# A graph-attention kernel: two result banks in turn, split operands for the small sums, and an earlier low part on GpSimd

## The reference

```python
# first layer (H is 1024 nodes x 64 hyperedges, 0 or 1; a node is in about 3)
h = x @ W
alpha = softmax(where(H.T > 0, leaky_relu(h @ a_node)[:, None, :], -1e9), -1)
agg = einsum('ben,bnf->bef', alpha, h)
beta = sigmoid((h @ a_gn)[:, None, :] + (agg @ a_ge)[:, :, None])
all_he = elu(beta[..., None] * h[:, None] + (1 - beta[..., None]) * agg[:, :, None])
se = tanh(elu(agg) @ fcW + fcb) @ av
coefs1 = softmax(where(H > 0, se[:, None, :], -1e9), -1)
g = einsum('bne,benf->bnf', coefs1, all_he)
...
# third layer (w: a 3 x 64 x 64 weight for each of 16 embedding directions)
w = einsum('nd,dkio->nkio', embedding, weight)
x_g = einsum('knm,bmc->bnkc', A_stack, x)
out = einsum('bnki,nkio->bno', x_g, w) + embedding @ bias
```

## Time and profile before

| | |
|---|---|
| median of 3 runs | 732.07 us |
| profiled execution | 729.97 us, of which 728.2 us is the span |
| TensorE busy | 665.5 us (91%) |
| VectorE, ScalarE, GpSimd busy | 421.7, 337.2, 289.7 us |
| first round starts, last round ends | about 102.8 us, 195.8 us |
| third layer's products (L1503) | 490.6 to 643 us |

### The profile page before, as it was taken

How to read it: one execution, slowest core, us unless ns; L and a number is a source line. 1 busy time by engine, 2 the same in 40 slices (tenths; PEclk the granted TensorE clock), 3 DMA queues, 4 the chain that set the end, 5 groups by cost and what they waited for, 6 DMA issues and landing times.

```text
span 728.2 us, 9826 instructions
## 1 busy us (share of the span) xinstructions
PE 665.5 (91%) x3420; PEld 460.7 (63%) x3428; DVE 421.7 (58%) x970; ACT 337.2 (46%) x645; POOL 289.7 (40%) x267
## 2 busy tenths in 40 slices
PE   6898988878799889999999999999999989899993
PEld 2796766656566767533333358887776767678883
DVE  1676656777439942466877856114565757561166
ACT  1861234544367442356566544413446565355214
POOL 0270105565526810001424257024667676760045
PEclk9999999999989799999999999999999999999998
DMA  9120030000000036000100000000000000000013
GB/s 329 34 87 2 1 116 1 1 0 1 2 1 1 4 79 153 1 0 1 59 0 1 1 1 1 1 0 1 2 1 1 0 1 1 1 1 2 1 28 88
DMA packets 14995, 18.34 MB, mean 25 GB/s; under 512 B 10128, under 2 KB 10128, under 8 KB 14944
## 3 DMA queue, kind: packets, MB, share of 16 engines
q1 hardware_dynamic: 14432, 16.06, 7.7%
q10 hardware_dynamic: 512, 1.60, 0.6%
HBM read 11.37 MB, written 2.10 MB: 18 GB/s over the span
## 4 chain that ended last, share of the span: by engine, by line
PE 53%; DVE 7%; POOL 7%; ACT 3%; issue 2%; ACTq 0%; POOLq 0%; DVEq 0%
PE PS L1503 8%; PE PS L1390 7%; PE PS L1373 7%; PE PS L1516 5%; PE PS L1556 4%; PE PS L1545 4%; POOL LN_Y L163 3%; DVE arena L2139 2%; PE PS L182 2%; PE PS L1482 2%; PE PS L1489 2%; PE PS L189 2%; PE PS L1566 2%; DVE LN_ST L140 2%; PE PS L1252 1%
## 5 line engine op out<-in xcount | busy, mean ns | idle before, releaser
L2139 DVE SCALAR_TENSOR_TENSOR arena<-PS,WT,arena 128x256 f32<-128x256 f32 x160 | 77.4, 484 | 59.2 <-PE PS L1516 34.6
L1713 ACT ACTIVATE arena<-PS,spare 128x1024 f32<-128x1024 f32 x64 | 70.8, 1109 | 49.8 <-DVE spare L2076 49.6
L1503 PE MATMUL PS<-WH,KK 128*128 128x512 f32 x256 | 87.2, 404 | 6.1 <-POOL KK L1917 5.6
L2076 DVE TENSOR_REDUCE spare<-PS 128x1 f32<-128x1024 f32 x64 | 75.6, 1219 | 23.8 <-PE PS L1373 23.7
L163 POOL TENSOR_TENSOR LN_Y<-LN_V,CN 128x16 f32<-128x16 f32 (+1 forms) x18 | 49.4, 2745 | 73.7 <-DVE LN_V L155 73.7
L1781 ACT ACTIVATE spare<-PS,WT 128x256 f32<-128x256 f32 x96 | 38.8, 472 | 68.5 <-DVE arena L2139 66.7
L1873 POOL TENSOR_TENSOR arena<-arena,spare 128x128 f32<-128x128 f32 x32 | 13.9, 433 | 134.7 <-DVE spare L2082 124.0
L1390 PE MATMUL PS<-arena 128*64 128x512 f32 x256 | 62.0, 605 | 1.5 <-POOL arena L1873 1.4
L1503 PEld LDWEIGHTS PS<-WH,KK 128*128 128x128 f32 x256 | 48.0, 188 | 24.0 <-issue 12.4
L1503 PE MATMUL PS<-WL,KK 128*128 128x512 f32 x128 | 50.1, 391 | 0.0
L1373 PE MATMUL PS<-arena 64*128 64x512 f32 x192 | 48.2, 618 | 1.4 <-ACT arena L1713 1.4
(11 more groups left out here) (293 smaller groups left out, 1491.8 us busy)
## 6 DMA issues: line engine op xcount, KB each, us to landing
arena<-in_adj_tr SPq DMA_DIRECT2D x8, 512.0 KB, 5.8
arena<-in_x_tr SPq DMA_DIRECT2D x4, 512.0 KB, 7.9
arena<-in_x_nat SPq DMA_DIRECT2D x1, 2048.0 KB, 9.2
arena<-arena SPq DMA_DIRECT2D x7, 256.0 KB, 2.8
arena<-arena SPq DMA_DIRECT2D x12, 128.0 KB, 2.3
spare<-in_w SPq DMA_DIRECT2D x2, 512.0 KB, 4.1
out<-arena SPq DMA_DIRECT2D x4, 256.0 KB, 3.0
out<-arena SPq DMA_DIRECT2D x8, 128.0 KB, 2.2
```

What stands on the lines that cost most here:

```text
L1503: ins = pe.matmul(acc, x[:, t % 2, b, :], w[:, k, c], start=(first and n == 0), stop=(not first and n == 2), skip_group_check=True)
L1713: act.activation(EF[2 * (i % RING) + par], banks("S", 2 * i + par).rearrange("p a c -> p (a c)"), ACT.Exp, bias=NMX[:, i, par:par + 1], ac ...
L2076: dve.tensor_reduce(NMX[:, i, par:par + 1], banks("S", 2 * i + par), AX.XY, ALU.max, negate=True).then_inc(max_ready, 1)
L2139: dve.scalar_tensor_tensor(acc, PS[:, four_banks(t, j), d * F:(d + 1) * F], WT[:, e:e + 1], acc, ALU.mult, ALU.add).then_inc(acc_step, 1)
```

## The change

It has five parts. (1) The sums of a tile go to bank 4 or 7 in turn (`sums_bank`), and TensorE waits for the copy of the tile before last. The denominators move to bank 5 and are added up round by round: ScalarE copies them to `ZR` when the round is done, GpSimd adds `ZR` to `ZS`. (2) In a round, `gather(t, C_)` comes ahead of `edge_rows`, and VectorE shifts chunk A ahead of `from_first`. (3) `small_sums` uses float32r operands with high and low part side by side (`SMR`, `HMR`): six products of 36 and 32 columns, whose halves are added by a `tensor_reduce`. (4) `NSF` becomes a float32r tile. (5) In the third layer's loop `low_parts(t + 1)` is issued ahead of `scales`.

```diff
-        NSF = arena[:, 4 * SLOT + CHUNKS * BF:4 * SLOT + CHUNKS * BF + ROUND].rearrange("p (c n) -> p c n", n=P)
+        NSF = rounded("NSF", 4 * SLOT + CHUNKS * BF, [P, CHUNKS, P])
...
+        SMR = nc.alloc_sbuf_tensor_at("SMR", [P, 2, 18], F32R, offset=spare_at + 4 * (2 * N + ROUND))
+        HMR = nc.alloc_sbuf_tensor_at("HMR", [P, NT, 2, 16], F32R, offset=spare_at + 4 * (2 * ROUND))
...
-        SMALL_AT, ZN_AT = CHUNKS * E, 0
+        SMALL_AT, ZN_AT = CHUNKS * E, 3 * P
+        ZR = sb("ZR", [P, B])
+        zr_out, zs_added = sem("zr_out"), sem("zs_added")
+
+        def sums_bank(t):
+            return 4 + 3 * (t % 2)
+
...
+        def small_parts(c):
+            return PS[:, 5, SMALL_AT + 36 * c:SMALL_AT + 36 * c + 36].rearrange("p (h k) -> p h k", k=18)
...
+                        pool.wait_ge(zr_out, j + 2)
+                        pool.tensor_tensor(ZS[:, t, :], ZS[:, t, :], ZR[:, :], ALU.add).then_inc(zs_added, 1)
                     if t + 2 < NT:
                         low(t + 2)
                     if t >= 1:
...
+                act.activation(ZR[:, :], zero16[:, 0:B], ACT.Copy).then_inc(zr_out, 1)
...
+                        act.wait_ge(acc_done, j + 2)
+                        act.activation(ZR[:, :], PS[:, 5, ZN_AT:ZN_AT + B], ACT.Copy).then_inc(zr_out, 1)
                     if t + 2 < NT:
                         high(t + 2)
-                    act.wait_ge(acc_done, first[t + 1] + 1)
-                    act.activation(GN[:, t, :], PS[:, 4, :], ACT.Copy)
-                    act.activation(ZS[:, t, :], PS[:, 7, ZN_AT:ZN_AT + B], ACT.Copy).then_inc(acc_out, 1)
+                    act.activation(GN[:, t, :], PS[:, sums_bank(t), :], ACT.Copy).then_inc(acc_out, 1)
...
+                    parts = PS[:, 5, SMALL_AT:SMALL_AT + 36 * CHUNKS].rearrange("p (c h k) -> p c h k", h=2, k=18)[:, :, :, 0:17]
+                    dve.tensor_reduce(TS[:, :, :], parts.rearrange("p c h k -> p c k h"), AX.X, ALU.add).then_inc(ts_ready, 1)
...
+                link(dve.tensor_copy(SMR[:, :, 17:18], zero16[:, 0:2].unsqueeze(2)))
+                link(dve.tensor_copy(SMR[:, 0, 0:17], SM[:, :]))
+                dve.tensor_tensor(SMR[:, 1, 0:17], SM[:, :], bits(SMR[:, 0, 0:17]), ALU.subtract)
...
-                ins.then_inc(hm_ready, 1)
+                link(ins)
+                dve.wait_ge(hg_out, 1)
+                link(dve.tensor_copy(HMR[:, :, 0, :], HM[:, :, 0:2 * B]))
+                dve.tensor_tensor(HMR[:, :, 1, :], HM[:, :, 0:2 * B], bits(HMR[:, :, 0, :]), ALU.subtract).then_inc(hm_ready, 1)
...
+                        shift(A_, 2)
                         dve.wait_ge(selg_ready, j + 1)
                         dve.wait_ge(nt_ready, j + 1)
                         from_first(at).then_inc(ns_half, 1)
-                        shift(A_, 2)
...
-                        dve.wait_ge(acc_out, t)
+                        dve.wait_ge(zs_added, first[t])
...
+                dve.wait_ge(zs_added, first[NT])
...
+                        acc = small_parts(c)
+                        pe.matmul(acc, SELF[:, c, :], SMR[:, :, :], start=True, stop=False, skip_group_check=True)
+                        ins = pe.matmul(acc[:, :, 0:16], NSF[:, c, :], HMR[:, bass.ds(t, 1), :, :].rearrange("p t h k -> p (t h) k"),
+                                        start=False, stop=True, skip_group_check=True)
...
-                    if t >= 1:
-                        pe.wait_ge(acc_out, t)
-                    pe.matmul(PS[:, 4, :], zero16[:, 0:P], zero16[:, :], start=True, stop=False, skip_group_check=True)
-                    pe.matmul(PS[:, 7, ZN_AT:ZN_AT + B], zero16[:, 0:P], zero16[:, 0:B], start=True, stop=False, skip_group_check=True)
+                    if t >= 2:
+                        pe.wait_ge(acc_out, t - 1)
+                    pe.matmul(PS[:, sums_bank(t), :], zero16[:, 0:P], zero16[:, :], start=True, stop=False, skip_group_check=True)
                     pe.wait_ge(hpl_ready, min(t + 2, NT))
                     with pe.Fori(first[t], first[t + 1]) as j:
                         k_next, t_next = next_round(j, t, first)
 
...
-                            return pe.matmul(PS[:, 4, :], NST[:, c, :], S1[:, c, :], start=False, stop=True, skip_group_check=True)
-
+                            return pe.matmul(PS[:, sums_bank(t), :], NST[:, c, :], S1[:, c, :], start=False, stop=True, skip_group_check=True)
+
+                        pe.wait_ge(z_ready, CHUNKS * j + 1)
+                        gather(t, C_)
+                        pe.wait_ge(zr_out, j + 1)
                         pe.wait_ge(ns_ready, j + 2)
                         edge_rows(t_next)
-                        pe.wait_ge(z_ready, CHUNKS * j + 1)
-                        gather(t, C_)
                         pe.wait_ge(nst_out, j + 1)
...
-                            ins = pe.matmul(PS[:, 7, ZN_AT:ZN_AT + B], NST[:, c, :], CC[:, c, :], start=False, stop=True,
-                                            skip_group_check=True)
+                            ins = pe.matmul(PS[:, 5, ZN_AT:ZN_AT + B], NST[:, c, :], CC[:, c, :], start=(c == 0),
+                                            stop=(c == CHUNKS - 1), skip_group_check=True)
                         ins.then_inc(acc_done, 1)
...
                     add_scaled(t, 0)
+                    if t + 1 < NT:
+                        low_parts(t + 1)
                     for i, (first, n) in enumerate(NORMS):
                         if first + n == t:
                             scales(i)
                     if t + 1 < NT:
-                        low_parts(t + 1)
                         init(t + 1)
                     add_scaled(t, 1)
                     combine(t)
```

More of the change, by code:

```diff
@@ L353, in _ @@
                 pool.memset(zero16[:, :], 0.0).then_inc(zero_set, 1)
+                pool.memset(ZS[:, :, :], 0.0)
                 pool.wait_ge(sl, 1)
@@ L497, in nodes_copy @@
                 def nodes_copy():
-                    act.activation(NSG[:, :, :], NSF[:, :, :], ACT.Copy).then_inc(nsg_ready, 1)
+                    act.activation(NSG[:, :, :], bits(NSF[:, :, :]), ACT.Copy).then_inc(nsg_ready, 1)
                 def tanh():
@@ L622, in to_last @@
                 def to_last(at):
-                    return dve.scalar_tensor_tensor(NSF[:, :, :], iota, HIT[:, bass.ds(at, 1)], NSF[:, :, :], ALU.is_lt, ALU.mult)
+                    return dve.scalar_tensor_tensor(NSF[:, :, :], iota, HIT[:, bass.ds(at, 1)], bits(NSF[:, :, :]), ALU.is_lt, ALU.mult)
                 def edges(k):
@@ L632, in small_out @@
                 def small_out():
-                    dve.tensor_copy(TS[:, :, :], PS[:, 5, SMALL_AT:SMALL_AT + 17 * CHUNKS].rearrange("p (c k) -> p c k", k=17)).then_inc(ts_ready, 1)
+                    parts = PS[:, 5, SMALL_AT:SMALL_AT + 36 * CHUNKS].rearrange("p (c h k) -> p c h k", h=2, k=18)[:, :, :, 0:17]
+                    dve.tensor_reduce(TS[:, :, :], parts.rearrange("p c h k -> p c k h"), AX.X, ALU.add).then_inc(ts_ready, 1)
                 def logits():
@@ L924, in edge_rows @@
                     for c in range(CHUNKS):
-                        ins = pe.matmul(PS[:, 5, c * E:(c + 1) * E], NSF[:, c, :], P1[:, bass.ds(t, 1), :], start=True, stop=True)
+                        ins = pe.matmul(PS[:, 5, c * E:(c + 1) * E], bits(NSF[:, c, :]), P1[:, bass.ds(t, 1), :], start=True, stop=True)
                     ins.then_inc(r_ready, 1)
@@ L929, in turn_nodes @@
                     for c in range(CHUNKS):
-                        ins = pe.transpose(PS[:, 6, tile(c)], NSF[:, c, :], ident)
+                        ins = pe.transpose(PS[:, 6, tile(c)], bits(NSF[:, c, :]), ident)
                     ins.then_inc(nt_ready, 1)
@@ L939, in small_sums @@
                     for c in range(CHUNKS):
-                        acc = PS[:, 5, SMALL_AT + 17 * c:SMALL_AT + 17 * c + 17]
-                        pe.matmul(acc, bits(SELF[:, c, :]), SM[:, :], start=True, stop=False, skip_group_check=True)
-                        ins = pe.matmul(acc, NSF[:, c, :], HM[:, bass.ds(t, 1), :], start=False, stop=True, skip_group_check=True)
+                        acc = small_parts(c)
+                        pe.matmul(acc, SELF[:, c, :], SMR[:, :, :], start=True, stop=False, skip_group_check=True)
+                        ins = pe.matmul(acc[:, :, 0:16], NSF[:, c, :], HMR[:, bass.ds(t, 1), :, :].rearrange("p t h k -> p (t h) k"),
+                                        start=False, stop=True, skip_group_check=True)
                     ins.then_inc(small_ready, 1)
```

## The result

The changed kernel takes 760.65 us (median of 4 runs, 760.45 to 768.42) against 732.08 for the one before: ratio 1.042, 95% interval 1.035 to 1.049. I had forecast 736.3 with a range up to 741. The direction was right; the size was not, by 24 us. The profiled execution took 760.61 us, its span is 758.8, and its granted clock 0.931 on average where the kernel before had 0.972.

What follows compares the result with a forecast made beforehand. TensorE sets the pace from `turn_edges` on, before it a chain through VectorE. Terms 0.4 - 0.6 + 1.5 + 7.2 + 0 + 1.3 - 5.6 = +4.2 on 732.07 gave 736.3 us, range 731.5 to 741.

Steps and rivals of the forecast that it cites:

- Direction and cause of the wait: At the seam of tiles 1 to 6, `low` waits behind GpSimd's add, so `turn_edges` starts 1.56 us later; total slower.
- sum of +4.2: All terms before, in and after the rounds and in the third layer: 4.2 us slower, median 736.3.
- rival 1: TensorE's clock in the rounds: no slow stretches -4 us (732.3), chance 0.12; five or six +3 to +4 (740).
- more slow rounds: Five or six rounds with a slow clock, +3 to +4 us; chance 0.18 together with the third layer's lost gain.
- Small sums: In each round, six float32r records instead of twelve save 0.63 us.
- tile 1: Its round takes 12.1 us for 10.60, +1.5.
- Chunk A's weights: In tiles 2 to 6, `scatter(A_)` waits for GpSimd's weighting: +0.5 us a round, bounds 0.2 and 0.9.
- Tile 7: The last round, which has no `low` ahead, takes 10.5 us for 10.53: 0.
- Two banks and VectorE's order: In the rounds, the removed wait for copies was hidden under `to_last` and TensorE is held by `low`: both worth nothing.
- Before the rounds: Five small VectorE instructions ahead of `hm_ready`, partly given back by the shorter `small_sums(0)`: +0.4 us (0 to 0.6).
- After the rounds: GpSimd's add, scaling and sum come ahead of the next block's barrier: +1.3 us (1.0 to 1.5).
- Third layer: TensorE's three waits for GpSimd's low part go: -5.6 us, or -3.5 if GpSimd's unchanged finish holds VectorE's statistics.

Runs made afterwards that it cites:

- both pauses filled: Changed kernel with nine products of zeros ahead of `gather` C and five behind `edge_rows`: 732.44 us, ratio 1.002 over the kernel before.
- zeros ahead of `turn_edges` alone: Changed kernel with five products of zeros behind `edge_rows` and none ahead of `gather` C: 739.56 us, ratio 1.015 over the kernel before.
- Part 2 alone: Kernel before with only `gather` C moved ahead of `edge_rows` and chunk A's shift ahead of `from_first`: 734.58 us, ratio 1.002.
- -5.8 alone: Kernel before with only the third layer's `low_parts(t + 1)` issued ahead of the power: 724.14 us, ratio 0.993.

## Why the prediction was right or wrong

- **Direction and cause of the wait: right.** `low` is held by the add, which waits for `ZR`; in the round shown `gather` C, `edge_rows` and `turn_edges` start within 0.13 us of where the prediction had them, and six waits of 2.2 to 2.4 us on `low` are in the trace.
- **The clock: wrong, and the whole miss.** The sum of +4.2 has no term for the clock, as if the slow stretches of the kernel before stayed as they were. The step that failed is the one that was to cover this, rival 1: "Five or six slow: +3 to +4", at 1.37 for each slow stretch. I saw that the pause gets as long or longer and that a second one comes, and then priced the stretch by the earlier trace rows, which show it behind the seam's pause alone. In the changed kernel it came in all seven rounds, and held for 10.3 us of the one shown, not 3.5; that round lost 16.54 - 12.57 = 4.0 us (2.5 to 4.9 over the seven). For tiles 1 to 7 the sum is 113.39 (after) against 87.16 (both pauses filled): 26.2 us, where the medians, each over the kernel before on its chip, differ by 26.3. With the price too low by a factor of 3, no chance given to "more slow rounds" could widen the range enough. What the lower level follows, other than that pauses of TensorE bring it, stays open.
- **Small sums: the record's price right, the gain wrong.** 0.63 shorter on TensorE, 0.29 on the path: `SELG` is late next. In the changed kernel it matters less, since `scatter(A_)` is late there anyway: 2.42 from `turn_edges` to `gather` B, where my steps had 2.34. In tile 1, which has no such wait, it is the better part of 12.6 against 12.1: 2.19 where my steps had 1.84 (zeros ahead of `turn_edges` alone, 12.59).
- **Chunk A's weights: right** for tiles 2 to 6. With both pauses filled `scatter(A_)` waits 0.4 us for them in five rounds; I had 0.5. The 0.9 that I had worked out for a `bend` late in full did not come, though `bend` took 1.39 there.
- **Tile 7: too low by 1.2.** 10.5 forecast. With both pauses filled it takes 11.72, but there nine zeros hold TensorE for 2 us that nothing else asks for. With zeros ahead of `turn_edges` alone it takes 11.70 at full clock, and the five zeros are done 0.57 us before `turn_edges` can start, so this is the schedule:

```profile
202.43 1.13 PE L1011 MATMUL PS<-arena 128*128 128x512 f32 x2 [1.48 <-POOL arena L389]
```

`scatter(A_)` waits 1.48 us for chunk A's weights and starts 5.42 behind zero, where my steps had the weights at 4.3: the add of the denominators ends at 0.85 and not 0.5, the sum of the tile before takes 1.62 and not 1.26, and the weighting, beside VectorE's `bend`, about 1.4 and not 1.04.
- **Two banks and VectorE's order: worth nothing, right** for the banks (their wait ended under `to_last`). Part 2 alone cost 0.14 a round in tiles 2 to 6 (11.29 for 11.15), and 0.6 and 0.7 in tiles 1 and 7.
- **Before the rounds:** -1.6 for +0.4. TensorE waited 0.41 us for the new VectorE instructions, as costed. The kernel before had a granted clock of 0.76 from 65 to 72 us, and the profiled run of the changed one had none there; with both pauses filled the first `gather` starts at 100.74 against 100.52, +0.2.
- **After the rounds:** +1.8 for +1.3; for half of it I had taken both engines' durations as alone, though the earlier trace rows show what they take beside each other.
- **Third layer: right**, -5.4 in the trace and -5.8 alone.

With the clock held (both pauses filled) the changed kernel takes 2.3 us more than the one before on the same chip. Rival 1 had +0.2 for a clock that stays full (732.3). The 2 us between are 1.2 in tile 7, 0.5 in tile 1 and 0.5 after the rounds. So the schedule was forecast within about 2 us, and the time missed by 24.

## What to carry to other kernels

A wait that TensorE gets has two prices: its length, and what the clock does to the work behind it. Cost the second by the rows of a slow round, but ask how the pauses add up in the new order; where they grow, the case "every round slow, for most of the round" is one to work out, not a rival's shade. Products of zeros into a bank that is open and awaited by nothing tell the two prices apart in one run, and can be left in.

Before an instruction with a new wait is put into an in-order list, look at what stands behind it. Here one add of 8 columns held the rows of the tile after next; moved behind the next round's `CC`, it turned the same change from 1.042 into 0.9955, and with zeros in the pause that was left into 0.984.
